# A decoder layer on one core: the first expert of the first half moved in front of the last batch's fifth score group, first weights prepared expert by expert, the second product by chunks

## The reference

```
x = x + self_attention(norm(x))          # 16 heads of 64, causal, softmax over the query axis
x = x + cross_attention(norm(x), ctx)    # 16 heads of 8, keys and values from ctx
x = x + experts(norm(x))                 # 8 experts, 2 picked for each row
# experts:
scores = x @ Wr + br;  weights = softmax of the best two scores, 0 elsewhere
for i in range(8):
    h = relu((x * picked[i]) @ W1[i] + b1[i])     # 128 -> 512
    out += (h @ W2[i] + b2[i]) * weights[i]       # 512 -> 128
```

## Time and profile before

| | us |
|---|---|
| median of 3 runs | 348.15 (346.92 to 350.82) |
| the profiled execution | 347.81 |
| its span, first to last instruction | 346.0 |
| TensorE busy | 301.5 (87%) |
| VectorE / ScalarE / GpSimd busy | 214.7 / 190.4 / 91.2 |
| mean granted TensorE clock | 0.975 |

### The profile page before, as it was taken

How to read it: one execution, slowest core, us unless ns; L and a number is a source line. 1 busy time by engine, 2 the same in 40 slices (tenths; PEclk the granted TensorE clock), 3 DMA queues, 4 the chain that set the end, 5 groups by cost and what they waited for, 6 DMA issues and landing times.

```text
span 346.0 us, 5393 instructions
## 1 busy us (share of the span) xinstructions
PE 301.5 (87%) x1852; PEld 212.2 (61%) x1869; DVE 214.7 (62%) x452; ACT 190.4 (55%) x525; POOL 91.2 (26%) x130
## 2 busy tenths in 40 slices
PE   6799999999988997988688367776999999799995
PEld 2677777767865784556234123334778678578884
DVE  4768563746488848745877267446766876556661
ACT  2679767478466634664365258684553454336350
POOL 7990550320112009302400490313421300000000
PEclk9999999999999998999899699999999999899999
DMA  8800035501000100010029920000000000100001
GB/s 244 175 2 2 2 52 67 66 3 45 0 2 13 35 1 3 3 46 2 3 64 366 282 72 4 2 0 2 0 1 2 0 1 0 32 0 0 3 0 30
DMA packets 14911, 14.06 MB, mean 41 GB/s; under 512 B 2643, under 2 KB 10915, under 8 KB 14883
## 3 DMA queue, kind: packets, MB, share of 16 engines
q1 hardware_dynamic: 13300, 12.92, 15.1%
q10 hardware_dynamic: 1584, 0.80, 0.8%
HBM read 9.94 MB, written 0.52 MB: 30 GB/s over the span
## 4 chain that ended last, share of the span: by engine, by line
PE 65%; DVE 16%; DMA 4%; ACT 4%; issue 3%; SPq 3%; POOL 2%; another core or an unknown queue 0%; DVEq 0%; ACTq 0%; POOLq 0%
PE ps L592 6%; PE ps L594 6%; PE ps L593 6%; PE ps L666 6%; PE ps L699 4%; PE ps L711 4%; PE ps L868 4%; PE ps L869 4%; PE ps L870 4%; DMA w_raw<-in_L_ffn_b 3%; PE ps L744 3%; DVE mneg L1233 3%; PE ps L780 3%; PE ps L673 2%; PE ps L701 2%
## 5 line engine op out<-in xcount | busy, mean ns | idle before, releaser
L987 ACT ACTIVATE p<-ps,negmax 128x256 f32<-128x256 f32 (+1 forms) x128 | 52.6, 425 | 26.5 <-DVE negmax L1202 26.2
L1314 DVE SCALAR_TENSOR_TENSOR hid_lo<-ps,hid_hi 128x512 fp32r<-128x512 f32 x64 | 41.8, 685 | 23.3 <-ACT hid_hi L1051 23.3
L1233 DVE TENSOR_REDUCE mneg<-ps 128x2 f32<-128x512 f32 x64 | 42.3, 683 | 21.6 <-PE ps L744 20.9
L1016 ACT ACTIVATE px<-ps 128x512 f32<-128x512 f32 x64 | 35.1, 598 | 23.9 <-PE ps L765 22.1
L1202 DVE TENSOR_REDUCE negmax<-ps 128x2 f32<-128x512 f32 (+1 forms) x48 | 33.0, 687 | 20.6 <-PE ps L668 13.2
L1051 ACT ACTIVATE hid_hi<-ps 128x512 fp32r<-128x512 f32 x64 | 35.0, 596 | 8.1 <-PE ps L594 7.6
L744 PE MATMUL ps<-k_st,q_mem 128*128 128x256 bf16 x128 | 25.5, 283 | 12.3 <-DVE mneg L1233 11.5
L1046 ACT CAST x_hi<-x_f 128x512 fp32r<-128x512 f32 x16 | 9.9, 620 | 38.8 <-DVE x_f L1304 38.8
L973 ACT CAST t_hi<-ps 128x512 fp32r<-128x512 f32 x32 | 18.7, 591 | 19.5 <-PE ps L594 18.5
L592 PE MATMUL ps<-x_hi,w_hi 128*128 128x512 f32 x64 | 26.4, 412 | 2.2 <-DVE hid_lo L1314 1.4
L987 ACT ACTIVATION_READ_ACCUMULATOR p<-ps,negmax 128x1 f32 x128 | 26.6, 208 | 0.0
...
## 6 DMA issues: line engine op xcount, KB each, us to landing
w_raw<-in_L_ffn_W SPq DMA_DIRECT2D x1, 2048.0 KB, 8.6
w_last<-in_L_ffn_W SPq DMA_DIRECT2D x1, 2048.0 KB, 14.5
...
```

What stands on the lines that cost most here:

```text
L987: last = act.activation(dst, bank[:, n * i:n * i + n], ACT.Exp, bias=negmax[:, kt, h:h + 1], accum_out=psums[:, kt, h:h + 1])
L1016: act.activation(px[:, (g // 2) % 2, c0:c0 + 512], ps[:, k % 3, :], ACT.Exp, scale=SCALE_X).then_inc(s_px, 1)
L1233: dve.tensor_reduce(mneg[:, qt, :].rearrange("p (r g) -> p r g", r=2)[:, :, g], ps[:, max_bank[("MX", b, u)], :].rearrange("p (h k) -> p h ...
L1314: dve.scalar_tensor_tensor(hid[1][:, k % 2, c, :], ps[:, H_BANK[c], :], 0.0, hid[0][:, k % 2, c, :].bitcast(F32), ALU.max, ALU.subtract).t ...
```

## The change

- The entries CS and CO of batch 3's groups 4 to 7 leave their own slots and stand between the chunks of slot k = 0, after H(0,0), H(0,1), H(0,2), H(0,3). `wo` and what follows for batches 2 and 3 moves to k = 1 and k = 2. In batch 2 the chain oq0 .. wo of batch 1 stands one slot earlier.
- `NT(0)` moves from slot (3,0) to (2,7), `RT` to (3,0), `GT` to (3,1), `WT` from (3,6) to (3,2), `X(0)` from (3,7) to (3,3).
- The last rows of the first weights come in eight loads of 256 KB into a ring of three. SyncE waits for `w1` and loads the bias row before `stack_m(2)`. `WS` entries are spread: (1,4), (1,6), (2,6), then k = 0 to 4, after chunk 0. `H(k,0)` waits for its own expert's low part alone. The low part moves from VectorE to GpSimd (`first_low`), which gets a new order.
- `W2(0)` stands in (3,2), `W2(k+1)` in slot k after chunk 2.
- Slot k is now X(k+1), then for c = 0 to 3: Y(k-1, c), H(k, c). `hid` has one buffer in place of two.
- Batch 3's scores use banks 0 and 1; the first two experts' H use banks 2 and 5; the two halves' output banks change places. Reads and writes of the hidden parts and banks follow these names in the rest of the diff, which is left out here. `weight_low` goes from VectorE.

```diff
@@ -264,11 +268,13 @@
         for b in range(B):
             units = [("oq0", b - 1), ("oT0", b - 1), ("oq1", b - 1), ("oT1", b - 1), ("wo", b - 1)] if b else \
                 [("V", last, 2), ("V", last, 3), ("Z", last, 2), ("Z", last, 3), ("PJ", last), ("n2T", last), ("q", last)]
+            if b == last:
+                units = [("oq0", b - 1), ("oq1", b - 1)]
             tail = {}
-            for g, unit in zip((2, 3, 4, 5, 5) if b else (0, 0, 1, 2, 3, 5, 6), units):
+            for g, unit in zip(((0, 0, 1, 2, 3, 5, 6), (2, 3, 4, 5, 5), (1, 2, 3, 4, 4), (1, 2))[b], units):
                 tail.setdefault(g, []).append(unit)
-            more = {(3, 0): [("NT", 0)], (3, 1): [("RT", 0)], (3, 3): [("GT", 0), ("W2", 0, 0)], (3, 5): [("W2", 0, 1)],
-                    (3, 6): [("WT", 0)], (3, 7): [("X", 0)]}
+            more = {(1, 4): [("WS", 0, 0)], (1, 6): [("WS", 0, 1)], (2, 6): [("WS", 0, 2)], (2, 7): [("NT", 0)],
+                    (3, 0): [("RT", 0)], (3, 1): [("GT", 0)], (3, 2): [("WT", 0), ("W2", 0, 0)], (3, 3): [("X", 0)]}
             for g in range(HP):
                 maxima_now, turn = max_plan.get((B + b, g), ([], []))
                 slot = [("CS", b, g, 0)] + maxima_now[:1] + [("CS", b, g, 1)]
...
@@ -279,24 +285,32 @@
                 if g == 0 and b >= 1:
                     slot += [("CO", b - 1, 3)]
                 slot += maxima_now[1:2] + (tail.get(g, []) if b else []) + maxima_now[2:] + more.get((b, g), []) + turn
-                if b == 2:
-                    slot += [("WS", 0, g)]
-                slots.append(slot)
-        slots.append([("CO", last, 3)])
-        beside = {(0, 0): [("oq0", last)], (0, 1): [("oT0", last)], (0, 2): [("oq1", last)], (0, 3): [("oT1", last)],
-                  (1, 0): [("wo", last)], (3, 1): [("NT", 1)], (4, 0): [("RT", 1)], (5, 1): [("GT", 1)],
-                  (6, 3): [("WT", 1)], (9, 0): [("YO", 0, 0)], (9, 1): [("YO", 0, 1)]}
-        for k in range(2 * NE):
+                if (b, g) < (last, 4):
+                    slots.append(slot)
+
+        beside = {(0, 0): [("CS", last, 4, 0), ("CS", last, 4, 1), ("CO", last, 1)],
+                  (0, 1): [("CS", last, 5, 0), ("CS", last, 5, 1)],
+                  (0, 2): [("CS", last, 6, 0), ("CS", last, 6, 1), ("CO", last, 2)],
+                  (0, 3): [("CS", last, 7, 0), ("CS", last, 7, 1), ("oT0", last - 1)],
+                  (1, 0): [("oT1", last - 1)], (1, 1): [("CO", last, 3), ("wo", last - 1)], (1, 3): [("oq0", last)],
+                  (2, 0): [("oT0", last)], (2, 1): [("oq1", last)], (2, 2): [("oT1", last)], (2, 3): [("wo", last)],
+                  (4, 2): [("NT", 1)], (5, 0): [("RT", 1)], (5, 2): [("GT", 1)],
+                  (6, 1): [("WT", 1)], (9, 1): [("YO", 0, 0)], (9, 2): [("YO", 0, 1)]}
+        for k in range(2 * NE + 1):
             slot = [("YE", 0, 0), ("YE", 0, 1)] if k == NE + 1 else []
             slot += [("X", k + 1)] if k + 1 < 2 * NE else []
             for c in range(NC):
-                slot += [("H", k, c)] + beside.get((k, c), [])
-            if k + 2 < NE:
-                slot += [("W2", 0, k + 2)]
+                slot += [("Y", k - 1, c)] if k else []
+                slot += [("H", k, c)] if k < 2 * NE else []
+                slot += beside.get((k, c), [])
+                if c == 0 and k + 3 < NE:
+                    slot += [("WS", 0, k + 3)]
+                if c == 2 and k + 1 < NE:
+                    slot += [("W2", 0, k + 1)]
             if k % NE == 2:
                 slot += [("B2", k // NE)]
-            slots.append(slot + ([("Y", k - 1)] if k else []))
-        slots.append([("Y", 2 * NE - 1), ("YE", 1, 0), ("YE", 1, 1), ("YO", 1, 0), ("YO", 1, 1)])
+            slots.append(slot)
+        slots.append([("YE", 1, 0), ("YE", 1, 1), ("YO", 1, 0), ("YO", 1, 1)])
         MISC = ("PJ", "n2T", "q", "mT", "oq0", "oT0", "oq1", "oT1", "wo", "NT", "RT", "WT", "YO")
         misc_at = {k: i for i, k in enumerate(k for slot in slots for k in slot if k[0] in MISC)}
         X_BANK = 6
...
+        def score_bank(b, k):
+
+            return k % 3 if b < B - 1 else k % 2
+
+        def out_bank(m):
+            return 3 + m % 2 if m < 2 * B - 1 else 3
+
+        def hidden_bank(k, c):
+            return (2, 5)[c % 2] if k < 2 else (0, 1, 2, 5)[c]
+
+        def last_in(bank, users):
+            return max((n for n, used in users if used == bank), default=-1)
+        score_banks = [score_bank(k // (2 * HP), k) for k in range(2 * HP * B)]
+        hidden_banks = [hidden_bank(n // NC, n % NC) for n in range(2 * NE * NC)]
 
         flat = [k for slot in slots for k in slot]
 
...
@@ -408,16 +437,27 @@
             sp.wait_ge(s_misc, misc_at[("PJ", B - 1)] + 1)
             sp.dma_start(w1_raw[:, :].rearrange("p (e n) -> p e n", n=HID), w1.rearrange("e p n -> p e n")
                          ).then_inc(s_w12[0], 16)
-            sp.dma_start(w1_last[:, :].rearrange("p (e n) -> p e n", n=HID), w1[:, LAST, :].partition_broadcast(P)
-                         ).then_inc(s_wlast, 16)
+
+            def last_rows(i):
+                if i >= LAST_RING:
+                    sp.wait_ge(s_wdiff, i - LAST_RING + 1)
+                sp.dma_start(w1_last[:, i % LAST_RING, :], w1[i, LAST, :].partition_broadcast(P)
+                             ).then_inc(s_wlast[i % LAST_RING], 16)
+
+            for i in range(LAST_RING):
+                last_rows(i)
             sp.wait_ge(s_zero, 1)
             for r in (0, LOW):
                 sp.dma_start(b2_sb[r:r + NE, :], b2).then_inc(s_b2, 16)
+            sp.wait_ge(s_w12[0], 16)
+            sp.dma_start(w1_raw[LAST:D, :], b1.rearrange("e n -> (e n)").unsqueeze(0)).then_inc(s_b1, 16)
             stack_m(2)
             sp.dma_start(w2_raw[:, :].rearrange("p (n d) -> p n d", d=D), w2.rearrange("e (c p) d -> p (e c) d", p=P)).then_inc(s_w12[1], 16)
-            sp.wait_ge(s_w12[0], 16)
-            sp.dma_start(w1_raw[LAST:D, :], b1.rearrange("e n -> (e n)").unsqueeze(0)).then_inc(s_b1, 16)
+            last_rows(3)
+            last_rows(4)
             stack_m(3)
+            for i in range(5, NE):
+                last_rows(i)
             for hf in range(2):
                 for i in range(2):
                     ts = slice(4 * hf + 2 * i, 4 * hf + 2 * i + 2)
...
@@ -514,10 +554,16 @@
             def first_weights(i):
                 if i == 0:
                     pool.wait_ge(s_w12[0], 16)
-                    pool.wait_ge(s_wlast, 16)
+                pool.wait_ge(s_wlast[i % LAST_RING], 16 * (i // LAST_RING + 1))
                 cols = slice(512 * i, 512 * i + 512)
-                pool.tensor_tensor(w1_raw[0:LAST, cols], w1_raw[0:LAST, cols], w1_last[0:LAST, cols], ALU.subtract
-                                   ).then_inc(s_wdiff, 1)
+                pool.tensor_tensor(w1_raw[0:LAST, cols], w1_raw[0:LAST, cols], w1_last[0:LAST, i % LAST_RING, :],
+                                   ALU.subtract).then_inc(s_wdiff, 1)
+
+            def first_low(i):
+                pool.wait_ge(s_whi, i + 1)
+                cols = slice(512 * i, 512 * i + 512)
+                pool.tensor_tensor(w1_lo[:, cols], w1_raw[:, cols], w1_hi[:, cols].bitcast(F32), ALU.subtract
+                                   ).then_inc(s_wlo, 1)
 
             def second_weights(i):
                 pool.wait_ge(s_w2hi, i + 1)
@@ -546,15 +592,29 @@
             pool.memset(wgt_p[:, :, :].bitcast(F32), 0.0).then_inc(s_pick, 1)
             pool.wait_ge(s_wr, 48)
             pool.tensor_tensor(wr_sb[0:LAST, :], wr_sb[0:LAST, :], wr_last[0:LAST, :], ALU.subtract).then_inc(s_pick, 1)
-            for i in range(NE):
-                first_weights(i)
+            first_weights(0)
+            first_weights(1)
             norm_3(0)
+            first_low(0)
+            first_weights(2)
+            first_low(1)
             norm_3(1)
+            first_weights(3)
+            first_low(2)
+            second_weights(0)
+            first_weights(4)
+            first_low(3)
             norm_3(2)
-            for i in range(3):
-                second_weights(i)
+            first_weights(5)
+            second_weights(1)
+            first_low(4)
             norm_3(3)
-            for i in range(3, NE):
+            for i in range(5, NE):
+                first_low(i)
+                if i + 1 < NE:
+                    first_weights(i + 1)
+                second_weights(i - 3)
+            for i in range(NE - 3, NE):
                 second_weights(i)
 
         @block.tensor
...
@@ -843,32 +903,35 @@
 
             def hidden(k, c):
 
-                e = k % NE
-                if k == 0 and c == 0:
-                    pe.wait_ge(s_wlo, 8)
-                    pe.wait_ge(s_px, 16 * B)
+                e, n = k % NE, NC * k + c
+                bank = hidden_banks[n]
+                if c == 0:
+                    if k < NE:
+                        pe.wait_ge(s_wlo, e + 1)
+                    pe.wait_ge(s_xlo, k + 1)
```

(48 more changed lines are left out.)

54 lines of the change are left out of this document (23 added, 31 removed).

## The result

The changed kernel takes 363.1 us (median of 4 runs, 359.73 to 363.69) against 347.53 for the kernel before: ratio 1.041, 95% interval 1.0315 to 1.0504. It is slower, as forecast, but by 4.1% instead of 1.2%, outside the range of 346 to 357 and above the 357 of rival 3. The profiled execution, the slowest of the four, took 363.69 with a span of 361.9 and a mean granted clock of 0.943, against 347.81, 346.0 and 0.975.

The account below looks back on a forecast made before the run. TensorE was taken as the bound in the experts, with gaps in cross attention. 4.3 ahead, 5.1 gained, 14.0 lost and 0.3 rounding made +4.2: 352.3 us, 1.2% slower; own range 350 to 355, 346 to 357 at 8 in 10.

Parts of the forecast that it names:

- rival 3: Slower, 357, chance 0.12: half rate from router product to K 1.5, port 1, third second-weights wait 1, bias row 2.
- K: Start of slot 1, forecast at 235.7, about 4.3 us ahead of before; over 3 us off would make the forecast wrong.
- chunks of Y: Second product by chunks in the experts: stalls 1.40 and 1.99 and the clock's 1.7 go, gain 5.1 us.
- the two stalls at Y: Before Y(1,0) and Y(2,0), second weights queue on GpSimd behind norms that wait for wo: 3.4 and 7.9 us.
- T to first H: From the router product's end through gates, divisions and WT to H(0,0): 9.7 us, first H at 227.9.
- first H to K (slot 0): Slot k = 0, bound by ScalarE with 8 us of work against TensorE's 6.8; K at 235.7.
- the new stall of 7.5: Before wo(0), behind ScalarE's first weight cast: about 7.5 us with half rate, replacing the 5.58 gap before 196.22.
- Rival 2: Faster, chance 0.12: second weights not late at Y(1,0) and Y(2,0), so 14.0 goes and the time is 338.3.
- another division 0.65: WT at T + 5.7: After the router product: VectorE's best-two, division 0.6, gates 2.35 and second division 0.65 put WT 5.7 us later.
- the port: GpSimd contends with VectorE for SBUF at low parts such as x_lo: 0.5 each, 1 us in all, left at 0.
- after 3.4 likelier than not, 1.0 as a mean: After the 3.4 us stall before Y(1,0): a clock fall costing 1.0 as a mean, bounds 0 and 1.7.
- last term of 83.25: From Y(2,0) at 262.75 to the output copy at 346.0: matmuls 77.4, extras 3.1, clock 1.75 + 1.0.

Follow-up runs that it names:

- e1: Changed kernel with only GpSimd's queue reordered, second_weights(1) and (2) ahead of norm_3(2) and norm_3(3): 345.86 us, ratio 0.996 to the kernel before.
- e2: Changed kernel with stack_m(2) issued before the wait for w1 and the first two WS entries moved to (2,1) and (2,3): 353.21 us, ratio 1.0175.
- e12: Changed kernel with only the first two WS entries moved to (2,1) and (2,3), stack_m(2) left late: 358.51 us, ratio 1.0294.
- e3: Changed kernel with oq1 of batch 2 moved one slot later, behind X(0): 358.48 us, ratio 1.0323.
- e13: e11 plus sixteen bf16 matmuls with unread results in TensorE's holes: 333.32 us, ratio 0.9581.
- e6: Kernel before with only the second product by chunks, Y(k-1,c) in front of H(k,c): 346.21 us, ratio 0.9966.
- e7: Changed kernel with the edits of e1, e2 and e3 together: 338.35 us, ratio 0.9765.
- e10: e7 with GpSimd kept off VectorE at x_lo, plus ScalarE's gates exponential moved from RT's place to GT's: 334.37 us, ratio 0.9626.
- e11: e10 with the second half's NT, RT, GT, WT moved forward to (4,0), (4,2), (5,0), (6,0): 335.29 us, ratio 0.963.
- e5: Changed kernel with front and GpSimd's queue mended, but batch 3's last four groups again in front of the experts: 337.43 us, ratio 0.9726.

## Why the prediction was wrong in size

The direction was right, and the deciding mechanism was named and timed: GpSimd's in-order queue behind wo. The end came 11.7 us later than the sum (357.69 against 346.0). One of the prediction's own signs of being wrong came true: K, forecast at 235.7, came at 240.36, 4.7 later where 3 was the limit. Two steps failed most: that chunks of Y would remove the second half's stalls and their clock (5.1), and that the clock would be low behind the two stalls at Y alone. Term by term, us from the profiled execution:

| term | forecast | measured | off |
|---|---|---|---|
| wo(0) starts | 193.7 | 193.22 | -0.5 |
| NT starts | 215.2 | 215.23 | 0 |
| T, end of RT | 218.2 | 218.28 | +0.1 |
| T to first H | 9.7 | 12.4 | +2.7 |
| first H to K (slot 0) | 7.8 | 9.65 | +1.85 |
| K to Y(1,0) | 11.45 | 11.54 | +0.1 |
| Y(1,0) to wo(3) | 6.2 | 8.24 | +2.0 |
| wo(3) to Y(2,0) | 9.4 | 9.13 | -0.3 |
| Y(2,0) to the output copy | 83.25 | 88.42 | +5.2 |

**Right.** The chain up to T, with the new stall of 7.5 (7.79 measured) in place of 5.58; both stalls at Y, 3.4 and 7.9 (3.08 and 7.43); and that the second is followed by half rate. e1, e2 and e12 show these as causes, by taking each away. Rival 2, the one on the other side, is out for the changed kernel, but its price was fair: with the queue mended alone the kernel gained 17.2, of which I had counted 14.0 to this cause.

**T to first H.** The step "another division 0.65: WT at T + 5.7" failed: WT ran at T + 7.45. The gates themselves were early, done at T + 4.74; WT waited for the division, whose input, the turn of `oq1`, lies in the bank that WT writes next:

```profile
222.83 0.19 DVE L1353 TENSOR_TENSOR wgt_p<-wgt,wgt_p 128x32 fp32r<-128x32 f32 x1
225.03 0.26 DVE L1309 RECIPROCAL r_den<-ps 128x16 f32<-128x16 f32 x1 [2.00 <-PE ps L850]
225.32 0.36 DVE L1313 TENSOR_TENSOR o_n<-ps,r_den 128x64 f32<-128x64 f32 x2
```

That turn was late on TensorE: in front of it stood 1.77 us of waiting for `px` and then a CO at half rate (1.94 instead of 1.07). e3 took 1.45 back by moving it. Then x_lo took 1.61 instead of 0.7. I had the row for this and set the term to 0 with the argument that VectorE idles during the long stall. That looked at the wrong place: the port bit here, on the chain.

**The clock.** I priced it as 1.75 + 1.0 behind the two stalls at Y. In the changed kernel it was low in three more stretches, 221.5 to 224.9 (in T to first H, above), 228.3 to 235.2 (slot 0, +1.85) and 296.6 to 300.0 (about 1.65). The step "after 3.4 likelier than not, 1.0 as a mean" was low too: the clock was at 0.83 in 250 to 260, and Y(1,0) to wo(3) took 2.0 longer. In TensorE's timeline, one kind of product in the stretch from 228.3 and behind it:

```profile
233.13 1.94 PE L840 MATMUL ps<-px,v_pad 128*32 128x256 f32 x16
...
238.09 1.07 PE L840 MATMUL ps<-px,v_pad 128*32 128x256 f32 x16
```

Rival 3 had this spell, with the port and the third wait for `w_lo` (0.82). I gave it 0.12 as something instead of the forecast; it came on top of it, and behind an argument ("ScalarE, not TensorE, is the bound there") that e13 refutes in the mended kernel.

**The gain of 5.1 by chunks.** This term of the sum failed worst. e6 gives 0.9 for it alone, and none of that in waits. In the changed kernel the two stalls of the earlier trace rows came back as 1.99 for the gates and 0.81 for `resid`, with a fall of the clock between. My argument compared VectorE's load with TensorE's slot; it didn't follow gates(1) to its own reader, WT(1), whose slot (6,1) had come nearer. The last term of 83.25 held 80.5 of work and the 2.75 of clock, of which 1.0 belonged two terms higher. Measured there: waits of 0.82 + 1.99 + 0.81 and spells of about 1.7 and 1.65, 7.0 together, which gives 87.5 of the 88.42. About 1.0 us stays unexplained.

**What made the change slower, then.** The medians are 15.6 us apart, and e1 returns 17.2 by one queue's order, 15.5 of it in the last stage. The front returns 9.9 in the median and 7.85 in its own stage, the gates' neighbours 1.45 in theirs. With all three mended (e7) the kernel is 9 us under the kernel before; the edits of e10, e11 and e13 together bring 5 more. The larger share is in the stretch ahead of NT (before 37.47, e5 28.72, e13 26.45), where the first weights come in parts and the casts leave batch 2; which of the two does it was not tested. The title's move is worth nothing measurable in one pair, and in the other pair its share of the 3.65 is not separated from the clock's and the exponential's.
